# A graph layer on one core: row sums per relation in three groups of relations instead of two

## The chip, the core and the metric

One core of a Trainium2 chip runs the whole layer in one launch. The metric is the device time of one execution in microseconds (us); lower is better. Engines are named as in the profile: PE (TensorE, matrix products), DVE (VectorE), ACT (ScalarE), POOL (GpSimd) and SP (SyncE), each with its own instruction stream in program order. Engines wait for one another on semaphores.

## The reference, cut to what matters

```python
N, D, R, E = 1250, 1024, 8, 20000
xn = layernorm(x)
# graph part: one mean over incoming edges for each of 8 relations
out = xn @ root + bias
for r in range(8):
    mask = (edge_type == r)
    sums = segment_sum(xn[src] * mask, dst, num_segments=N)
    cnt = segment_sum(mask, dst, num_segments=N)
    out = out + (sums / max(cnt, 1)) @ weight[r]
u = out
z = concat([u, xn]) @ w_gate + b_gate
h = tanh(u) * z + xn * (1 - z)
x = x + h + linear_attention(xn)
x = x + fp4_ffn(layernorm(x))       # weights and activations quantized in blocks of 16
```

Edges come sorted by destination. On average a node has 16 incoming edges, 2 per relation.

## The kernel before, in words

The product is turned round: for each relation r the kernel first computes y_r = xn @ weight[r] for all nodes and stores it to memory (`relation_rows`), and the row of node n in `out` is then the sum over its edges of the row `src` of y_r, times 1/cnt. So the sums over edges need rows of products that are already stored.

**Steps.** PE runs 210 column steps (`NSTEP`). Step n is one tile of 128 nodes (n mod 10) times one block of weight columns (h = n // 10): h = 0 is q, k, v; h = 1 to 16 are the 8 relations, two halves of 512 columns each; 17 and 18 are root; 19 and 20 are the x part of the gate. A step is 24 matmuls of 128x512 (L1791: three products of high and low parts, eight k). ACT copies each step's result to EV and issues its store (L2166, L2168); from step 190 on DVE does the copy, with a bias (L1590). SP loads the weight rows (RAW, a ring of 4), ACT makes their high part (L2144), POOL their low part (L843 in `low_rows`), at t = n mod 10 = 1 to 8 for the block after. The engines' other work is hung on these steps: each engine's stream is written out step by step, so step numbers set the order within each engine.

**Edges.** From steps 10 to 19 DVE computes for each edge its place in a table of columns (`edge_words`, `edge_places`, `run_counts`): its running number among the edges of the same node in the same group of relations, and for the ones that do not fit a place among the columns left over. PE helps with small transposes at fixed places (`RUNS_AT`). Then `bucket_totals` on DVE counts edges by group and tile, one one-hot comparison and one sum per group. After that DVE makes the features for the attention keys, which PE takes from step 20 on (L1874). POOL scatters the edges' words to a table in memory (L922), and loads it back at step 75 (`LISTS_AT`). From step 79 (`COUNT_FROM`) PE counts left-over edges, one small matmul per left-over column after each k (`count_left`, L1838). At step `COUNTED_AT` (88 before) POOL stores the counts (L948), waits for them, and fetches the weights 1/cnt of the left-over columns with one indirect DMA per column (L894, `fetch_weights`), two columns per step.

**Groups, planes and left-over columns.** The relations are cut in groups. In each group and tile of 128 nodes there are `PLANES` columns of own rows (column c holds the node's c-th edge of the group, so partition p is node p) and `OVER` columns left over (any 128 edges of that tile and group). A column is an *item*. Each item is one indirect gather of up to 128 rows of 4 KB by POOL (L901) into one of 4 slots of `source_rows` (`RING`). A missing edge has an index out of bounds and moves no row.

- A plane takes one DVE instruction (L1548): u_sum = row * weight + u_sum.
- A left-over column takes a one-hot on DVE (L1528), a high part on ACT (L2226, `left_over_hi`), a low part on DVE (L1532), and four matmuls of 128x512 on PE (L1918, `aggregate`), hung at the last k of the step after the item's own. That is where PE waits for the item. Its slot is free when PE is done.
- When a tile's items are done, DVE adds the PSUM sums (L1558, `finish`), SP stores u_sum at place 2 of the next tile (L693). In all groups but the first, SP loads the sum so far of a tile at place 5 of the tile ahead (L689). In the last group root rows are added too (L1563).

Item m of a group has the step `AGG_FROM[g] + index * steps // items`; its gather stands in POOL's stream at the step of item m-4, behind that step's `low_rows`, and waits until item m-4 has let go of the slot. The groups' starts are `AGG_FROM`; a group's first gathers stand two steps ahead and need the group's last relation stored.

Other work on DVE: from step 118 (`QUANT_FROM`) the feed-forward weights are quantized, 24 pieces, at steps 2, 3 and 5 of each 7, up to step 173.

After step 209: PE multiplies u by its gate weights (L2034), and then the quantized feed-forward follows.

Of the kernel before, what the change touches and what calls it, by code (L numbers as in the profile page):

```python
# [25 lines left out]
R = 8  # L26
# [6 lines left out]

GROUPS = ((0, 5), (5, R))
NG = len(GROUPS)
PLANES = (8, 5)
OVER = (3, 2)
NBK = NG * NT  # L40
NPL = sum(PLANES) * NT
NOV = sum(OVER) * NT
NCOL = NPL + NOV
PLANE0 = [sum(PLANES[:g]) * NT for g in range(NG)]
OVER0 = [NPL + sum(OVER[:g]) * NT for g in range(NG)]
GCB = (11, 7)
NCH = sum(GCB) * NT
CHUNK0 = [sum(GCB[:g]) * NT for g in range(NG)]
ROUNDS_MAX = -(-E // (min(GCB) * P))
# [23 lines left out]
NSTEP = NT * NH  # L73
# [24 lines left out]
LISTS_AT = 75  # L98
COUNT_FROM = 79
COUNTED_AT = COUNT_FROM - (-NOV // KT) + 2  # L100
AGG_FROM = (117, 178, NSTEP)
QUANT_FROM, QUANT_STEPS = 118, 7


# [57 lines left out]
def gps_layer(nc, x, src, dst, edge_type_8, weight, root, bias, w_gate, b_gate, gamma, w_q, w_kv,  # L162
              w_out, ff_gate, ff_up, ff_down, out):
    with ExitStack() as ctx:
# [10 lines left out]

        y_d = [nc.dram_tensor(f"relation_rows{a}", [(b - a) * NP, D], F32).ap() for a, b in GROUPS]
        u_d = nc.dram_tensor("u_rows", [NP, D], F32).ap()
# [24 lines left out]
        zeros16 = keep("zeros16", [P, P], F16)  # L202
        bucket_ids = keep("bucket_ids", [P, len(GROUPS), NT], F32)
        round_edges = keep("round_edges", [P, len(GROUPS), ROUNDS_MAX], F32)
        norms = keep("norms", [P, NT], F32)
# [28 lines left out]
        e_tot = keep("edge_totals", [P, NBK], F32)  # L234
        e_end = keep("edge_ends", [P, len(GROUPS), NT + 1], F32)
        e_off = keep("edge_offsets", [P, NBK], F32)
# [113 lines left out]
        rc_out = sem("rc_out")  # L350
        weights_in = [sem(f"weights_in{j}") for j in range(len(GROUPS))]

# [460 lines left out]
        def _(pool):  # L813
# [114 lines left out]
            w_next = 0  # L928
            c_next = 0
            for n in range(NSTEP + 1):  # L930
                h, t = n // NT, n % NT
                if 1 <= t <= KT and n < NSTEP:
                    low_rows(KT * (h + 1) + t - 1)
                if n == SCATTER_FROM:
                    pool.wait_ge(words_ready, 1)
                if n >= SCATTER_FROM:
                    for c in range(c_next, min(c_next + SCATTER_EACH, EC)):
                        scatter(c)
                    c_next = min(c_next + SCATTER_EACH, EC)
                if n == LISTS_AT:  # L940
                    pool.wait_ge(mix_ps, NT)
                    for k in range(NLIST):
                        pool.wait_ge(listed[k], 16 * (EC // NLIST + 1))
                        g.dma_start(LISTS[:, k, :], list_d[k].rearrange(
                            "(p c) a -> p (c a)", p=P)).then_inc(lists_in, 16)
                if n == COUNTED_AT:
                    pool.wait_ge(lists_done, 1)
                    g.dma_start(rc_d.rearrange("(p c) a -> p (c a)", p=P), rcnt[:]).then_inc(rc_out, 16)  # L948
                    pool.wait_ge(rc_out, 16)
                if n >= COUNTED_AT:  # L950
                    for q in range(w_next, min(w_next + 2, NOV)):
                        fetch_weights(NPL + q, weight_at, q).then_inc(
                            weights_in[max(k for k in range(NG) if NPL + q >= OVER0[k])], 16)
                    w_next = min(w_next + 2, NOV)
                if n == AGG_FROM[0] - 2:
                    pool.wait_ge(mix_ps, NT)
                    g.memset(XG[:].rearrange("p s d -> p (s d)").bitcast(F32), 0.0).then_inc(xg_zero, 1)
                    pool.wait_ge(xg_zero, 1)
                for m in GATHERS_AT[n]:
                    gather(m)  # L960
# [1450 lines left out]
```

## Time and profile before

| | |
|---|---|
| runs | 1684.55, 1687.99, 1688.33 us; median 1687.99 |
| the profiled execution | 1685.22 us, of which its span is 1683.5 us |
| busy in the span | PE 1564.9 us (93%), DVE 902.8 (54%), POOL 784.0 (47%), ACT 403.2 (24%) |
| waits of PE, largest | 29.0 us for the low part of left-over columns (L1918, 18 times), 15.3 for hidden_t_lo, 12.3 and 12.1 for x at the start |
| DMA | 262.48 MB, mean 156 GB/s |

The profile counts an engine busy while an instruction of it is in work; matmuls overlap, so a busy PE hides gaps below about 0.2 us. PEclk is the granted clock of PE in tenths of full speed. Waits tell for whom an engine stood idle. Where the kernel is bound by PE, only time in which PE waits, runs at the lower clock, or has more matmuls counts.

### The profile page before, as it was taken

What the parts mean: (1) busy time and instruction counts of PE and PEld (TensorE: products, weight loads), DVE (VectorE), ACT (ScalarE), POOL (GpSimd) and SP (SyncE); (2) the same over time, 40 slices, a digit from 0 to 9 for tenths busy, and PEclk for the clock granted to TensorE, in tenths of its full rate; (3) what the DMA queues carried; (4) which work ended last, traced back from release to release, by engine and by line L of the source; (5) the groups of instructions that cost most, each with busy time, mean ns of one, the idle gap of its engine ahead of it and who ended that gap; (6) DMA issues with size and microseconds to landing.
All of it is one profiled execution on the core that took longest, in us unless ns stands there. A gap on an engine that the chain in (4) does not pass through costs nothing.

```text
span 1683.5 us, 19033 instructions
## 1 busy us (share of the span) xinstructions
PE 1564.9 (93%) x7138; PEld 1266.8 (75%) x7138; DVE 902.8 (54%) x1344; ACT 403.2 (24%) x595; POOL 784.0 (47%) x672
## 2 busy tenths in 40 slices
PE   4999999999999999999999999999899969977988
PEld 4987777777777688888778787777677758866887
DVE  6534223444432400006887788875677727777785
ACT  3321112222222121122222232232211122232220
POOL 4426766666662145644454464564555531211010
PEclk9999999999999999999999999999999979988999
DMA  4423333333323222237777777877887845440001
GB/s 156 141 93 83 84 91 85 110 99 98 104 89 101 76 85 82 94 116 236 256 256 246 245 254 260 264 244 254 319 272 270 296 179 189 151 136 7 31 38 47
DMA packets 120459, 262.48 MB, mean 156 GB/s; under 512 B 23451, under 2 KB 37010, under 8 KB 120360
## 3 DMA queue, kind: packets, MB, share of 16 engines
q1 hardware_dynamic: 48568, 109.34, 19.6%
q0 software_dynamic: 33056, 83.02, 16.5%
q10 hardware_dynamic: 38736, 68.83, 11.0%
q8 instruction: 58, 0.95, 0.2%
q14 instruction: 41, 0.34, 0.1%
HBM read 193.33 MB, written 80.06 MB: 162 GB/s over the span
## 4 chain that ended last, share of the span: by engine, by line
PE 62%; DVE 18%; DMA 9%; issue 5%; ACT 3%; POOL 2%; ACTq 0%; SPq 0%; POOLq 0%; DVEq 0%
PE ps L1791 46%; DMA source_rows<-relation_rows,row_list 6%; PE ps L2034 5%; DVE u_sum L1548 3%; PE ps L2066 2%; PE ps L1918 2%; PE ps L2084 2%; DVE source_rows L1532 1%; PE ps L1874 1%; PE ps L1898 1%; DMA u_sum<-u_rows 1%; PE ps L1910 1%; ACT source_rows_hi L2226 1%; DVE wq_rows L575 1%; DVE u_sum L1558 1%
## 5 line engine op out<-in xcount | busy, mean ns | idle before, releaser
L1791 PE MATMUL ps<-WH,XTH 128*128 128x512 f32 (+1 forms) x1680 | 667.0, 397 | 0.0
L1791 PE MATMUL ps<-WH,XTL 128*128 128x512 f32 (+1 forms) x1680 | 653.0, 389 | 0.0
L1791 PE MATMUL ps<-WL,XTH 128*128 128x512 f32 (+1 forms) x1680 | 652.7, 388 | 0.0
L1791 PEld LDWEIGHTS ps<-WH,XTH 128*128 128x128 f32 x1680 | 318.8, 190 | 65.1 <-issue 7.1
L843 POOL TENSOR_TENSOR WL<-RAW,WH 128x512 fp32r<-128x512 f32 (+1 forms) x184 | 239.1, 1303 | 275.8 <-ACT WH L2144 273.5
L1791 PEld LDWEIGHTS ps<-WH,XTL 128*128 128x128 f32 x1680 | 316.9, 189 | 64.5
L1791 PEld LDWEIGHTS ps<-WL,XTH 128*128 128x128 f32 x1680 | 317.7, 189 | 60.5 <-issue 2.4
L901 POOL DMA_INDIRECT source_rows<-relation_rows,row_list x180 | 223.3, 1241 | 265.7 <-PE ps L1918 119.4
L2166 ACT ACTIVATE EV<-ps 128x512 f32<-128x512 f32 x180 | 107.2, 595 | 582.7 <-PE ps L1791 511.1
L922 POOL DMA_INDIRECT edge_lists<-edge_words x160 | 196.9, 1231 | 46.3 <-issue 44.6
L1548 DVE SCALAR_TENSOR_TENSOR u_sum<-source_rows,weight_list,u_sum 128x1024 f32<-128x1024 f32 x120 | 169.8, 1415 | 77.4 <-DMA source_rows<-relation_rows,row_list 70.2
L1532 DVE SCALAR_TENSOR_TENSOR source_rows<-source_rows,weight_list,source_rows_hi 128x1024 fp32r<-128x1024 f32 x50 | 77.5, 1550 | 218.6 <-ACT source_rows_hi L2226 218.5
L2144 ACT ACTIVATE WH<-RAW 128x512 fp32r<-128x512 f32 (+1 forms) x184 | 115.1, 627 | 159.1 <-DVE EV L1590 74.7
L2226 ACT ACTIVATE source_rows_hi<-source_rows,weight_list 128x1024 fp32r<-128x1024 f32 x50 | 57.4, 1149 | 168.3 <-DMA source_rows<-relation_rows,row_list 138.2
L1493 DVE TENSOR_TENSOR prefix<-ps,qkv_tile 128x544 f32<-128x544 f32 x40 | 29.0, 724 | 110.5 <-PE ps L1898 110.5
L1009 POOL TENSOR_TENSOR xf<-xf,edge_words 128x1024 f32<-128x1024 f32 x10 | 19.4, 1940 | 138.2 <-DVE xf L1699 138.2
L2034 PE MATMUL ps<-WH,TH 128*128 128x512 f32 x160 | 65.6, 410 | 10.2 <-DVE TL L1649 10.2
L2034 PE MATMUL ps<-WL,TH 128*128 128x512 f32 x160 | 64.4, 402 | 0.0
L2034 PE MATMUL ps<-WH,TL 128*128 128x512 f32 x160 | 64.3, 402 | 0.0
L1918 PE MATMUL ps<-source_rows_hi,edge_one_hots 128*128 128x512 f32 x100 | 33.8, 420 | 29.1 <-DVE source_rows L1532 29.0
L894 POOL DMA_INDIRECT weight_list<-edge_weights,weight_at x50 | 50.2, 1005 | 15.4 <-issue 9.4
L1452 DVE COPY values<-qkv_tile 128x128 f32<-128x128 f32 x10 | 2.3, 227 | 93.2 <-PE ps L1878 93.1
(312 smaller groups left out, 1550.2 us busy)
## 6 DMA issues: line engine op xcount, KB each, us to landing
relation_rows<-EV ACTq DMA_DIRECT2D x160, 256.0 KB, 2.2
RAW<-in_L_gnn_weight SPq DMA_DIRECT2D x128, 256.0 KB, 2.9
u_rows<-u_sum SPq DMA_DIRECT2D x20, 512.0 KB, 5.4
RAW<-in_L_gnn_w_gate SPq DMA_DIRECT2D x32, 256.0 KB, 4.6
mix_rows<-mix_rows_out ACTq DMA_DIRECT2D x10, 512.0 KB, 2.6
root_rows<-EV ACTq DMA_DIRECT2D x20, 256.0 KB, 4.6
u_sum<-u_rows SPq DMA_DIRECT2D x10, 512.0 KB, 6.9
bias_rows<-root_rows SPq DMA_DIRECT2D x10, 512.0 KB, 7.0
```

What stands on the lines that cost most here:

```text
L843: g.tensor_tensor(WL[:, h % 2, k, 0:w], RAW[:, q % 4, 0:w], WH[:, h % 2, k, 0:w].bitcast(F32), ALU.subtract).then_inc(w_lo, 1)
L894: return g.indirect_dma_start(out=weight_list[:, to:to + 1], out_offset=None, in_=rc_d, in_offset=bass.IndirectOffsetOnAxis(ap=places[:, a ...
L901: return g.indirect_dma_start(out=XG[:, slot, :].bitcast(F32), out_offset=None, in_=y_d[group], in_offset=bass.IndirectOffsetOnAxis(ap=row ...
L922: g.indirect_dma_start(out=list_d[k], out_offset=bass.IndirectOffsetOnAxis(ap=ew[0:EP, SLOT, c:c + 1].bitcast(U32), axis=0), in_=ew[0:EP, ...
L1532: v.scalar_tensor_tensor(rows_, rows_.bitcast(F32), weight_list[:, m.column:m.column + 1], OHI[:].bitcast(F32), ALU.mult, ALU.subtract).th ...
L1548: v.scalar_tensor_tensor(acc[:], XG[:, m.index % RING, :].bitcast(F32), weight_list[:, m.column:m.column + 1], base[:], ALU.mult, ALU.add) ...
L1791: mm = t_.matmul(ps[:, bank, 0:w], a[:, t, k, :], b[:, s, k, 0:w], start=(k == 0 and j == 0), stop=(k == KT - 1 and j == 2))
L1918: mm = t_.matmul(ps[:, bank + b, :], S1H[:, one_hot, :], part[:, 512 * b:512 * b + 512], start=(first and j == 0), stop=(last and j == 1))
L2034: mm = t_.matmul(ps[:, 4 + 2 * s + b, :], a[:, s, k, :], w[:, h % 2, k, :], start=(k == 0 and j == 0), stop=(k == KT - 1 and j == 2))
L2144: a.activation(WH[:, h % 2, k, 0:w], raw, ACT.Copy).then_inc(w_hi, 1)
L2166: a.activation(ev_slot(s), ps[:, prod_bank(n), :], ACT.Copy).then_inc(ev, 1)
L2226: a.activation(OHI[:], XG[:, slot, :].bitcast(F32), ACT.Copy, scale=weight_list[:, m.column:m.column + 1]).then_inc(oh_hi, 1)
```

## The change

There are three groups of relations, 0 to 3, 4 to 5 and 6 to 7, with 8, 5 and 5 planes and 2, 1 and 1 left-over columns for each tile. Before there were two, 0 to 4 and 5 to 7, with 8 and 5 planes and 3 and 2 left over. So there are 180 planes and 40 left-over columns, 220 items, where there were 130, 50 and 180. The first group starts at step 93 instead of 117, the middle one at 147, the last one at 178 as before. Left-over weights are fetched four columns per step. `COUNTED_AT` follows from the number of left-over columns and becomes 86. `GCB` is a size of a general path that runs only when the edges do not fit the columns; the edges of the inputs fit in both versions (most left over in one tile and group: 177 of 256, 69 of 128 and 65 of 128; before 347 of 384 and 229 of 256).

```diff
--- before.py
+++ after.py
@@ -33,17 +33,17 @@
 
 
 
-GROUPS = ((0, 5), (5, R))
+GROUPS = ((0, 4), (4, 6), (6, R))
 NG = len(GROUPS)
-PLANES = (8, 5)
-OVER = (3, 2)
+PLANES = (8, 5, 5)
+OVER = (2, 1, 1)
 NBK = NG * NT
 NPL = sum(PLANES) * NT
 NOV = sum(OVER) * NT
 NCOL = NPL + NOV
 PLANE0 = [sum(PLANES[:g]) * NT for g in range(NG)]
 OVER0 = [NPL + sum(OVER[:g]) * NT for g in range(NG)]
-GCB = (11, 7)
+GCB = (9, 5, 6)
 NCH = sum(GCB) * NT
 CHUNK0 = [sum(GCB[:g]) * NT for g in range(NG)]
 ROUNDS_MAX = -(-E // (min(GCB) * P))
@@ -98,7 +98,7 @@
 LISTS_AT = 75
 COUNT_FROM = 79
 COUNTED_AT = COUNT_FROM - (-NOV // KT) + 2
-AGG_FROM = (117, 178, NSTEP)
+AGG_FROM = (93, 147, 178, NSTEP)
 QUANT_FROM, QUANT_STEPS = 118, 7
 
 
@@ -948,10 +948,10 @@
                     g.dma_start(rc_d.rearrange("(p c) a -> p (c a)", p=P), rcnt[:]).then_inc(rc_out, 16)
                     pool.wait_ge(rc_out, 16)
                 if n >= COUNTED_AT:
-                    for q in range(w_next, min(w_next + 2, NOV)):
+                    for q in range(w_next, min(w_next + 4, NOV)):
                         fetch_weights(NPL + q, weight_at, q).then_inc(
                             weights_in[max(k for k in range(NG) if NPL + q >= OVER0[k])], 16)
-                    w_next = min(w_next + 2, NOV)
+                    w_next = min(w_next + 4, NOV)
                 if n == AGG_FROM[0] - 2:
                     pool.wait_ge(mix_ps, NT)
                     g.memset(XG[:].rearrange("p s d -> p (s d)").bitcast(F32), 0.0).then_inc(xg_zero, 1)
```

**POOL, from the store of the counts to the first gathers.** Weight fetches are `weight_list<-edge_weights`, row gathers `source_rows<-relation_rows`, `WL<-RAW,WH` the low parts of weight rows. Before, at step 88 and at the end of the fetches, and then the first gathers of step 115:

```order
 L948 DMA edge_weights<-rcnt 128x80
 L894 DMA weight_list<-edge_weights,weight_at 128x1 x6
 L843 TENSOR_TENSOR WL<-RAW,WH 128x512
 L894 DMA weight_list<-edge_weights,weight_at 128x1 x2
 L843 TENSOR_TENSOR WL<-RAW,WH 128x512
 L894 DMA weight_list<-edge_weights,weight_at 128x1 x2
```

Now, from step 86 to step 96:

```order
 L948 DMA edge_weights<-rcnt 128x80
 L894 DMA weight_list<-edge_weights,weight_at 128x1 x4
 L843 TENSOR_TENSOR WL<-RAW,WH 128x512
 L894 DMA weight_list<-edge_weights,weight_at 128x1 x4
 L843 TENSOR_TENSOR WL<-RAW,WH 128x512
 L894 DMA weight_list<-edge_weights,weight_at 128x1 x12
 L843 TENSOR_TENSOR WL<-RAW,WH 128x512
 L894 DMA weight_list<-edge_weights,weight_at 128x1 x4
 L957 MEMSET source_rows 128x4096
 L901 DMA source_rows<-relation_rows,row_list 128x1024 x4
 L843 TENSOR_TENSOR WL<-RAW,WH 128x512
 L894 DMA weight_list<-edge_weights,weight_at 128x1 x4
```

Before, the 50 fetches were done long ahead of the first gather; now 24 of the 40 stand right ahead of it and 16 in between the first ones.

**DVE, in the placement of the edges (steps 16 to 19).** Names: `prefix`, `onehot` and `edge_words` are tables of 125 x 160 edges; L1083 is the third group's term in a table by group, L1317 and L1328 the one-hot and the sum of one group. One piece of the difference:

```order
 L1194 SCALAR_TENSOR_TENSOR edge_words<-prefix,unsorted 125x160
 L1080 TENSOR_SCALAR edge_words<-edge_words 125x160
+L1083 SCALAR_TENSOR_TENSOR edge_words<-edge_words 125x160
 L1325 TENSOR_TENSOR edge_words<-edge_words 125x160
+L1317 TENSOR_TENSOR onehot<-edge_words,bucket_ids 125x1600
+L1328 TENSOR_REDUCE edge_totals<-onehot 125x10
 L1317 TENSOR_TENSOR onehot<-edge_words,bucket_ids 125x1600
```

Three instructions are added here, two of them over 1600 elements; earlier in the same part each loop over groups has one more pass.

## Rows read from the trace of the kernel before

**Rows 1.** The page's chain of work that ended last, shares by engine.
```profile
PE 62%; DVE 18%; DMA 9%; issue 5%; ACT 3%; POOL 2%; ACTq 0%; SPq 0%; POOLq 0%; DVEq 0%
```

**Rows 2.** Waits of PE: us in total, times, longest; whole span, then 1148 to 1350.
```profile
PE ps L1918 <- DVE source_rows L1532: 29.0, 18, 3.3
PE ps L1918 <- DVE source_rows L1532: 16.6, 11, 3.3
```

**Rows 3.** Timeline of ACT: start us, us; evacuations after steps 79, 83, 90, 117, 178.
```profile
545.24 0.60 ACT L2166 ACTIVATE EV<-ps 128x512 f32<-128x512 f32 x1 [6.01 <-PE ps L1791]
571.69 0.60 ACT L2166 ACTIVATE EV<-ps 128x512 f32<-128x512 f32 x1 [4.93 <-PE ps L1791]
612.04 0.60 ACT L2166 ACTIVATE EV<-ps 128x512 f32<-128x512 f32 x1 [4.84 <-PE ps L1791]
758.92 0.60 ACT L2166 ACTIVATE EV<-ps 128x512 f32<-128x512 f32 x1 [2.57 <-PE ps L1791]
1137.56 0.60 ACT L2166 ACTIVATE EV<-ps 128x512 f32<-128x512 f32 x1 [2.71 <-PE ps L1791]
```

**Rows 4.** Timeline of DVE and PE, end of the edge placement.
```profile
116.45 0.55 DVE L1140 TENSOR_TENSOR_SCAN prefix<-prefix,run_carry 125x160 f32<-125x160 f32 x1
117.48 0.49 DVE L1143 TENSOR_TENSOR prefix<-prefix 125x320 f32<-125x320 f32 x1
126.37 0.32 DVE L1187 SCALAR_TENSOR_TENSOR prefix<-edge_words 125x160 f32<-125x160 f32 x1
130.33 1.83 DVE L1317 TENSOR_TENSOR onehot<-edge_words,bucket_ids 125x1600 f32<-125x1600 f32 x1
132.20 1.82 DVE L1328 TENSOR_REDUCE edge_totals<-onehot 125x10 f32<-125x1600 f32 x1
139.93 0.44 PE L1874 MATMUL ps<-onehot,qkv_tile 128*32 128x289 f32 x2 [0.59 <-DVE onehot L456]
```

**Rows 5.** Timeline of POOL: counts stored, weights fetched, first row gathers.
```profile
598.22 0.56 POOL L948 DMA_DIRECT2D edge_weights<-rcnt  x1
602.14 1.06 POOL L894 DMA_INDIRECT weight_list<-edge_weights,weight_at  x1 [3.37 <-DMA edge_weights<-rcnt]
603.51 1.02 POOL L894 DMA_INDIRECT weight_list<-edge_weights,weight_at  x1 [0.30 <-issue]
613.82 1.29 POOL L843 TENSOR_TENSOR WL<-RAW,WH 128x512 fp32r<-128x512 f32 x1 [4.07 <-ACT WH L2144]
745.59 3.53 POOL L957 MEMSET source_rows<- 128x4096 f32 x1
749.89 1.01 POOL L901 DMA_INDIRECT source_rows<-relation_rows,row_list  x1 [0.77 <-POOL source_rows L957]
```

**Rows 6.** Timeline of DVE and PE, first left-over column.
```profile
756.38 2.07 DVE L1532 SCALAR_TENSOR_TENSOR source_rows<-source_rows,weight_list,source_rows_hi 128x1024 fp32r<-128x1024 f32 x1 [153.15 <-ACT source_rows_hi L2226]
764.16 0.39 PE L1918 MATMUL ps<-source_rows_hi,edge_one_hots 128*128 128x512 f32 x1
```

**Rows 7.** Instructions of source_rows: ns min/median/max; waiters; landing times.
```profile
L901 POOL DMA_INDIRECT source_rows<-relation_rows,row_list x180: 986/1008/2056, 749.9 to 1340.3; - x180
L1548 DVE SCALAR_TENSOR_TENSOR u_sum<-source_rows,weight_list,u_sum x120: 1267/1285/3044, 763.9 to 1348.8; 128x1024 f32<-128x1024 f32 x120
...
  POOL source_rows L901: 239.8, 77
...
DMA to landing us min/median/max: 3.2/5.9/10.7
```

**Rows 8.** Windows of 10 us: busy (x) by engine, PEclk, DMA share, GB/s.
```profile
805.00:815.00 10.00, 7.62 (x27) 5.79 (x26) 6.25 (x7) 1.85 (x4) 5.88 (x6) 0.83 0.93 307
```

**Rows 9.** Window of DVE: length, busy (x), PEclk, DMA share, GB/s.
```profile
765.00:970.00 205.00, 160.64 (x217) 0.98 0.76 246
```

**Rows 10.** Timeline of PE and DVE, end of the last step.
```profile
1344.41 0.39 PE L1791 MATMUL ps<-WH,XTL 128*128 128x512 f32 x1
1350.01 0.68 DVE L1590 TENSOR_TENSOR EV<-ps,z_bias 128x512 f32<-128x512 f32 x1
```

## The prediction

> **What bounds the kernel now.** I read the chain of work that ended last first. PE carries 62% of it and nothing else more than 18% [rows 1], so a change counts by what PE does, waits for, or runs slower at. The waits of PE come next: the largest are 29.0 us, 18 times, up to 3.3 us, for the low part of a left-over column [rows 2]. That is the one place at which the sums over edges hold PE. Then the marks of the steps in ACT's timeline. From step 90 to 117 PE needs (758.92 - 612.04)/27 = 5.44 us a step [rows 3], with nothing to wait for: the plain price of a step, 24 matmuls of 0.227 us. From 117 to 178 it takes 378.64 us for 61 steps. The plain price is 331.8, and the 30 left-over columns have four matmuls each, 0.91 us, 27.3 in all, so 19.5 us are lost. From 178 to the last product at 1344.6 [rows 10] there are 31 steps, 168.6 us, and 20 columns, 18.1, of 207.1 us: 20.4 lost. So 39.9 us are lost while items run. 29.0 are the waits, and the rest is mostly the clock: in the 10 us from 805 PE waited 2.4 us and the granted clock was 0.83 [rows 8], a level of 1.2 GHz for part of that window, which is 1.7 us more; I count four windows like it, some 7 us.
>
> Why the waits: a left-over column keeps its slot until the end of the step after its own. POOL stands at the gather of item m+4 until then (in all it was held 239.8 us in 77 places by source_rows [rows 7]), and that gather lands 5.9 us (median) later. When item m+4 is itself left over, it reaches PE just in time or late. Before, two of three left-over columns in the first group and half in the second follow at distance 4 (places 0, 3, 7 of 11; 0, 3 of 7).
>
> **The change part by part**, against the profiled execution's 1685.2 us (span 1683.5).
>
> *Placement of the edges, DVE.* What comes before DVE's last wait for PE in this part is hidden: DVE stood idle there. After it, at 116.3, all is in one line, and PE takes the first key features at 139.93 after 0.59 us of waiting [rows 4]: the line has no slack. The third group adds one scan pass (a scan is 0.55, some 0.5 in line), four instructions over all groups' elements that grow by half (0.49 for 320 elements, so about 0.17 each), one more multiply-compare (0.3), five L1083 (each 0.32 and a semaphore, 0.36, by L1187), and one pair L1317 and L1328 (1.83 + 1.82, 3.7 with gaps). Sum 0.5 + 0.7 + 0.3 + 1.8 + 3.7 = 7.0, with loose ends 7.1 us. All of it becomes a wait of PE at step 20. Next late: nothing, since in the key steps DVE idles until PE is done with each tile. **+7.1.**
>
> *Counting left-over edges.* Steps with these matmuls take (571.69 - 545.24)/4 = 6.61 us [rows 3], 1.17 over the plain price for eight: 0.146 each. Ten fewer: **-1.5.** The longer tables (220 columns for 180) add a microsecond to DVE before PE's first count, and PE did not wait there.
>
> *Matmuls of left-over columns.* Ten fewer at 0.91 us (PE's four from 764.16 [rows 6]): **-9.1.** Fifty more planes are DVE's, 40 more gathers POOL's. The rows moved stay one per edge, 20000 of 4 KB; only ten more loads and stores each of u_sum are added, over 117 steps instead of 93. So transfers per step fall, and I take landing times as before.
>
> *The start of the first group.* This is the queue of POOL. Let T be the start of step 86. POOL reaches the store of the counts at T + 3.0, and the first weight fetch comes 3.9 us later [rows 5], at T + 6.9. A fetch takes 1.31 us in line (1.02 and a gap of 0.30), a low part 1.29 and 1.43 with the gap behind it. Four fetches end at T + 12.2; steps 87 and 88 with a low part and four fetches add 6.65 each, to 25.5; steps 89 and 90 add 5.2 each, to 35.9; step 91 to 42.6. The memset and its wait are 4.3 (745.59 to 749.89), so the first gather is issued at T + 46.9. Before, from that issue to the end of the low part took 8.6 us (749.89 to 756.38 + 2.07 [rows 5, 6]), which gives T + 55.5. PE is at that column's place nine steps after T, at 49.0: it waits 6.5. Before, the same column was ready at 758.45 and PE came at 764.16. Behind the four gathers (52.1) stand steps 92 and 93 with eight more fetches (65.4) and then gathers 4 and 5. Item 5 is left over: issued 66.7, ready 75.3, PE there at 59.8 + 0.9 + 6.5 = 67.2, so it waits 8.1. Steps 94 and 95 bring POOL to 86.4, gather 10 goes out at 87.8, ready 96.4, PE there at 76.2 + 1.8 + 14.6 = 92.6: 3.8. After that POOL has 1.4 + 2 x 1.3 = 4.0 us of work in a step of 5.44 and catches up; item 15 is in time. Sum **+18.4.** With the shortest landing (3.2 against the 5.3 assumed) it is 16.3, with the longest (10.7) 23.8 [rows 7].
>
> POOL's gather instruction has a median of 1.008 us and a maximum of 2.056 [rows 7]; at the start DVE has little to do, and I priced it at the quiet pitch. The Trainium skill, "GPSIMD Engine Reference", section Specifications, says that GpSimd shares its SBUF interface with VectorE and contends with DVE instructions that read two SBUF inputs. The plane's multiply-add is one, and the change adds fifty. By the quiet row the start costs 18.4; by the rule, with each of the ten gathers concerned half way to the maximum of its row, it would be 5 more.
>
> *Waits while items run.* After the start 37 left-over columns remain. In the second and third group they are 6 items apart, 3.1 steps: the late item m+4 lands about 3.3 steps after m, and item m+6 is due at PE 5 steps after, nearly a step of slack. In the first group they are 5 apart; where that falls on two steps (about six times) the slack is about 1.5 us, otherwise a step more. The nearest rows are 16.6 us in 20 columns, 0.83 each, for the last group before, and with the other 12.4 in 30, 0.41 each, for the first [rows 2]. The bounds are 0 and 0.83 each: 0 to 31 us. I take 0.25, 9 us: six tight columns at the old rate or a little more, and some for the middle stretch, where DVE is fullest. 9 for 29: **-20.**
>
> *Clock.* Four waits of over 3 us (step 20 and the start) and one later at 1.7 us, against four before: **+1.7.**
>
> *The last step.* PE's last product ended at 1344.6, but DVE put its copy behind the last planes, which waited for their gathers, until 1350.01 [rows 10]; the rest hangs on that copy's store. With 1.9 items a step for 2.2 these gathers come in time: at most 5.1 us gained, I take **-4.**
>
> Sum: 1685.2 + 7.1 - 1.5 - 9.1 + 18.4 - 20 + 1.7 - 4 = 1677.8. The profiled execution lies 2.8 us below the median of the runs, and 1.3 below the mean of all four. I forecast 1679 us.
>
> **The rivals.**
> *DVE becomes the bound in the middle stretch (slower).* Between 765 and 970 DVE was busy 160.64 of 205 us [rows 9], 4.9 us in a step of 6.2. From step 147 to 173 a step has 0.14 more items (0.2 us) and 0.16 more tile ends (0.2): 5.25 us for a step that should take 5.73. It decides from the point where quantization, which comes in bursts, holds DVE for more than the one step of slack. Then the old rate of 0.83 us per column goes on: 31 us instead of 9, 1700 us. For it: 92% load. Against it: a step more of slack than before at a similar load.
> *Half of the waits stay (no change).* 19 us instead of 9, by late loads of u_sum, which now have two items of time (5.9 us) between issue and use, where three were: 1688.
> *The start costs nothing (much faster).* If POOL gets to the first gathers in time, 18.4 and the three clock windows (5.1) fall away: 1654. Against it stand 24 fetches at a measured pitch in front of them.
>
> **How the numbers follow.** A measurement of this kernel tells about 0.3%, 5 us, from no change. My forecast has 0.49, DVE as the bound 0.25, half of the waits 0.18, the free start 0.08. The forecast's own range is 1665 to 1683: waits of 0 and 15, a start of 16.3 and 23.8. For 8 in 10 I take 1662 to 1700: it leaves out most of the free start and the part of the slow case above 1700. Faster by over 0.3%: 0.57; within: 0.18; slower: 0.25.
>
> **What would show it.** The first wait of PE at L1874 is 7 to 8 us. Three waits at L1918 of about 6.5, 8 and 4 us lie at steps 95 to 100, with POOL never idle between the first weight fetch and gather 10. Later waits at L1918 sum to about 9. The last copy by DVE starts within 2 us of PE's last product. I am wrong if the waits between steps 147 and 178 exceed 8 us, if ACT or the weight rows (w_lo) hold PE after the start, or if the first gather goes out before step 94.

## The result, and the profile after

| | before | after |
|---|---|---|
| median of five runs | 1687.99 us (1678.0 to 1690.69) | 1701.53 us (1698.17 to 1704.51) |
| ratio to before | | 1.0086, 95% interval 1.0066 to 1.0105 |
| profiled execution, and its span | 1685.22, 1683.5 us | 1704.51, 1702.6 us |

The changed kernel is 0.9% slower. The forecast was 1679 us in a range of 1662 to 1700, so it had the wrong sign, and the time lies above the range. The profiled executions are 19.3 us apart, the medians 13.5, since the one of before was a little fast and the one of after a little slow; the working below is in profiled executions.

I read the new profile in the order of the old one. First the page's chain of work that ended last, by engine:

```profile
PE 49%; DVE 21%; DMA 10%; issue 10%; POOL 7%; ACT 3%; ACTq 0%; SPq 0%; POOLq 0%; DVEq 0%
```

PE had 62% of it [rows 1]. It now has 49%, and what took its place is POOL, DVE, transfers, and "issue", time in which an engine waited for nothing that the profile shows. The clearest place is the start: from 550 to 700 the chain was PE alone before, and now has 21% in POOL's weight fetches and 22% in "issue".

Then the waits of PE (total, times, longest), in the whole span, then the stretches 643 to 700, 795 to 976, 976 to 1175 and 1175 to 1369, that is the start of the first group, its rest in steps 118 to 146, and the second and third group:

```profile
PE ps L1918 <- DVE source_rows L1532: 47.7, 20, 6.0
PE ps L1874 <- DVE onehot L456: 6.7, 1, 6.7
...
PE ps L1918 <- DVE source_rows L1532: 15.5, 3, 6.0
...
PE ps L1918 <- DVE source_rows L1532: 7.8, 5, 3.8
...
PE ps L1918 <- DVE source_rows L1532: 18.1, 6, 6.0
...
PE ps L1918 <- DVE source_rows L1532: 6.3, 6, 2.1
```

There are 40 left-over columns for 50, but 47.7 us of waiting for them instead of 29.0 [rows 2].

Then the marks of the steps: ACT's evacuations after steps 79, 117 and 178, and DVE's last copy.

```profile
552.41 0.60 ACT L2166 ACTIVATE EV<-ps 128x512 f32<-128x512 f32 x1 [6.01 <-PE ps L1791]
794.66 0.60 ACT L2166 ACTIVATE EV<-ps 128x512 f32<-128x512 f32 x1 [0.82 <-PE ps L1791]
1180.59 0.60 ACT L2166 ACTIVATE EV<-ps 128x512 f32<-128x512 f32 x1 [1.76 <-PE ps L1791]
...
1368.87 0.68 DVE L1590 TENSOR_TENSOR EV<-ps,z_bias 128x512 f32<-128x512 f32 x1
```

Set beside the same marks of before [rows 3, 10], they say where the 19.1 us of span went:

| stretch | before | after | difference |
|---|---|---|---|
| start to step 79 | 545.2 | 552.4 | +7.2 |
| 79 to 117 | 213.7 | 242.3 | +28.6 |
| 117 to 178 | 378.6 | 385.9 | +7.3 |
| 178 to the last copy | 212.5 | 188.3 | -24.2 |
| behind it | 333.5 | 333.7 | +0.2 |

The last stretch gained 24 us, as was hoped: 9 of them are the matmuls of ten left-over columns, 10 are waits. The edge placement and the start of the first group took 36, and the middle, which should have given back, took 7 more. The second and third rows hide a shift: nine left-over columns, 8 us of matmuls, now stand before the mark of step 117. Without it the start lost some 22 us and the stretch from 117 to 178 some 15.

### The profile page after: what moved, and what is told of

Same layout as the page of the kernel before. It is cut to its first block, busy times and chain, and to the rows that moved or that the text cites. A ratio compares the mean times of both kernels' runs of the same rounds, so it can differ in the third digit from the quotient of the medians.

```text
span 1702.6 us, 19114 instructions
## 1 busy us (share of the span) xinstructions
PE 1560.4 (92%) x7088; PEld 1262.4 (74%) x7088; DVE 984.5 (58%) x1392; ACT 392.8 (23%) x585; POOL 827.9 (49%) x703
## 4 chain that ended last, share of the span: by engine, by line
PE 49%; DVE 21%; DMA 10%; issue 10%; POOL 7%; ACT 3%; ACTq 0%; SPq 0%; POOLq 0%; DVEq 0%
PE ps L1791 35%; PE ps L2034 5%; DMA source_rows<-relation_rows,row_list 4%; DVE u_sum L1548 3%; DMA u_sum<-u_rows 3%; POOL WL L843 2%; POOL source_rows L901 2%; PE ps L2066 2%; POOL weight_list L894 2%; PE ps L1874 1%; PE ps L1918 1%; PE ps L2084 1%; PE ps L1898 1%; DVE wq_tmp L565 1%; PE ps L1910 1%
## 5 line engine op out<-in xcount | busy, mean ns | idle before, releaser
L901 POOL DMA_INDIRECT source_rows<-relation_rows,row_list x220 | 269.0, 1223 | 302.2 <-DVE u_sum L1548 138.4
L1548 DVE SCALAR_TENSOR_TENSOR u_sum<-source_rows,weight_list,u_sum 128x1024 f32<-128x1024 f32 x170 | 242.1, 1424 | 136.1 <-DMA source_rows<-relation_rows,row_list 97.0
L1532 DVE SCALAR_TENSOR_TENSOR source_rows<-source_rows,weight_list,source_rows_hi 128x1024 fp32r<-128x1024 f32 x40 | 69.0, 1726 | 102.1 <-ACT source_rows_hi L2226 102.1
L2226 ACT ACTIVATE source_rows_hi<-source_rows,weight_list 128x1024 fp32r<-128x1024 f32 x40 | 46.0, 1150 | 156.0 <-DMA source_rows<-relation_rows,row_list 156.0
L1918 PE MATMUL ps<-source_rows_hi,edge_one_hots 128*128 128x512 f32 x80 | 28.5, 439 | 47.7 <-DVE source_rows L1532 47.7
L1918 PEld LDWEIGHTS ps<-source_rows_hi,edge_one_hots 128*128 128x128 f32 x80 | 14.1, 198 | 57.3 <-issue 41.6
```

The costliest lines, as they stand in the source:

```text
L901: return g.indirect_dma_start(out=XG[:, slot, :].bitcast(F32), out_offset=None, in_=y_d[group], in_offset=bass.IndirectOffsetOnAxis(ap=row ...
L1532: v.scalar_tensor_tensor(rows_, rows_.bitcast(F32), weight_list[:, m.column:m.column + 1], OHI[:].bitcast(F32), ALU.mult, ALU.subtract).th ...
L1548: v.scalar_tensor_tensor(acc[:], XG[:, m.index % RING, :].bitcast(F32), weight_list[:, m.column:m.column + 1], base[:], ALU.mult, ALU.add) ...
L1918: mm = t_.matmul(ps[:, bank + b, :], S1H[:, one_hot, :], part[:, 512 * b:512 * b + 512], start=(first and j == 0), stop=(last and j == 1))
L2226: a.activation(OHI[:], XG[:, slot, :].bitcast(F32), ACT.Copy, scale=weight_list[:, m.column:m.column + 1]).then_inc(oh_hi, 1)
```

## The experiments

Each is an edit of the changed kernel (e) or of the kernel before (b). Each batch was timed beside the kernel before on its chip, and comparisons go by the ratio to it: 0.001 is 1.7 us, and the changed kernel stands at 1.0086. A difference from the changed kernel joins two such ratios, each good to about 0.002, so it is uncertain by some 4 us. Waits are those of the one profiled execution of each kernel. An added line moves lines below it by one, so L1919 and L1533 in some profiles are L1918 and L1532 here.

**e1: fewer weight fetches ahead of the first gathers.** Once the weights of the first group's 20 left-over columns are in, one fetch per step.

```diff
-                    for q in range(w_next, min(w_next + 4, NOV)):
+                    some = 4 if w_next < NT * OVER[0] else 1
+                    for q in range(w_next, min(w_next + some, NOV)):
...
-                    w_next = min(w_next + 4, NOV)
+                    w_next = min(w_next + some, NOV)
```

> The changed kernel, with one edit: the 20 weights of the first group are fetched four per step as before, the 20 of the other two groups one per step after that. Theory POOL's queue: the first row gather is issued 5.2 - 1.3 = 3.9 us earlier, steps 92 to 95 of POOL are 3.9 us shorter each, so the first wait of PE at L1918 is about 0 (3.9 before), the next two (5.6 and 6.0) are gone, with the clock windows some 17 us of the 22.3 us lost in steps 86 to 102: 1685 us. Rival, that latency of the gathers themselves makes these waits: under 5 us gained.

Measured: 1683.74 us, ratio 0.9989 (0.9974 to 1.0004), so 16 us less than the changed kernel. POOL's first gather of the changed kernel and of this one:

```profile
636.03 1.00 POOL L901 DMA_INDIRECT source_rows<-relation_rows,row_list  x1 [0.77 <-POOL source_rows L957]
```

```profile
633.32 1.01 POOL L901 DMA_INDIRECT source_rows<-relation_rows,row_list  x1 [0.77 <-POOL source_rows L958]
```

It goes out 2.7 us sooner, and 4.2 counted from the start of step 86 (3.9 was expected), which takes away the first wait. The rest of the 16 us comes behind it, where single fetches stand between the gathers instead of groups of eight. PE waited 1.5 us where it had waited 15.5, and steps 86 to 102 took 97.6 us for 117.6. The middle and the end stayed much as they were (17.4 and 5.7 us of waits). The start is a loss of its own, of the size and from the queue that the prediction named.

**e2: quantization earlier,** in steps 91 to 146 instead of 118 to 173, so that it is over before the second group.

```diff
-QUANT_FROM, QUANT_STEPS = 118, 7
+QUANT_FROM, QUANT_STEPS = 91, 7
```

> The changed kernel, with one edit: quantization of the feed-forward weights runs from step 91 to 146 instead of 118 to 173, so the middle stretch (147 to 177) has none of it. Theory DVE's load: the 18.1 us of waits at L1918 in the middle stretch fall below 4, those in the first group after step 118 (7.8) stay or grow by some us, and the kernel is 8 to 14 us faster than the changed one: 1690 us. Rival, the loads of u_sum that stand behind weight rows on SP: the middle stretch keeps most of its 18.1 us, within 5 us of 1701.

Measured: 1686.57 us, ratio 1.0006 (0.9990 to 1.0022), 13.5 us less. Waits of PE in its steps 147 to 177 (978 to 1154):

```profile
PE ps L1918 <- DVE source_rows L1532: 1.3, 1, 1.3
```

and these steps took 175.9 us where they took 199.6. With DVE free the middle stretch is not late, though DVE waited longer there for loads of u_sum than in the changed kernel (15.1 us):

```profile
DVE u_sum L1548 <- DMA u_sum<-u_rows: 27.8, 9, 5.4
```

So late loads alone hardly reached PE in this run; in e6 below they cost more.

**e3: u_sum stored and loaded one place earlier by SP.** In the last group the load of the root rows stands with the store and moves too.

```diff
-                    if m.place == 2 and m.sum > 0:
+                    if m.place == 1 and m.sum > 0:
...
-                    if m.place == 5 and NT <= m.sum + 1 < NBK:
+                    if m.place == 4 and NT <= m.sum + 1 < NBK:
```

> The changed kernel, with one edit on SP: u_sum is stored at place 1 of the next tile and loaded at place 4 (2 and 5 before), one item earlier each. Theory late loads of u_sum: DVE's waits for them (11.1 us in the middle stretch, 18.9 in the last one) fall by half or more, the waits of PE in the middle stretch from 18.1 to under 10, 8 to 12 us faster than the changed one: 1691 us. Rival DVE's load by quantization: PE's waits stay within 3 us, 1700 us.

Measured: 1689.25 us, ratio 1.0022 (1.0007 to 1.0038), 10.8 us less. PE's waits in the middle fell from 18.1 to 11.1 us (under 10 was expected), those of the last group from 6.3 to none, and DVE's for u_sum from 15 to 3 and from 15 to 0.4. So the late loads do cost, in part of the middle and, with the root rows, in the last group.

**e4: only two groups' edge totals.** The third group's totals are set to zero instead of counted (its part of the table by tile is left out; the edges of these inputs fit and do not need it).

```diff
-                for j in range(NG):
+                v.memset(e_tot[0:EP, 2 * NT:3 * NT], 0.0)
+                for j in range(2):
...
-                    if j < NG - 1:
+                    if j < 1:
```

> The changed kernel without the count of edges of the third group (its totals are set to zero; they only decide whether the general path runs, so no output changes). One one-hot comparison and one sum less on DVE: the wait of PE at L1874 falls from 6.7 us by 3.7 to 3.0 if this line of DVE is all that PE waits for; if something else released it, it stays.

Measured: PE's wait for the first key features, of the changed kernel and of this one:

```profile
PE ps L1874 <- DVE onehot L456: 6.7, 1, 6.7
```

```profile
PE ps L1875 <- DVE onehot L456: 3.0, 1, 3.0
```

3.7 us, the price set for the pair L1317 and L1328 from [rows 4], to a tenth. Its one run took 1697.91 us, which alone is too near to the others' spread to show it.

**e5: the three edits together.**

> The changed kernel with all three edits together: one weight fetch per step once the first group's are in, quantization from step 91, and SP's store and load of u_sum one place earlier. Theory (three separate losses, each freed by its own edit): the start's loss falls from 22 to about 5 us (quantization now shares these steps, so not to 2), the waits of PE at left-over columns in steps 146 to 177 from 18 to about 1, and those of the last stretch from 6 to about 0; of the 48 us of waits less than 10 stay, and the time is 1660 us, 1655 to 1668. Rival (the losses are one slack passed on: what one edit frees, the next stage takes): at best the single edits' 1684 us, 1680 to 1687, with 25 us of waits or more left.

Measured: 1669.78 us, ratio 0.9900 (0.9873 to 0.9927). Faster than before, but 10 us short of the theory. The middle and the last group behaved (0 and 2.1 us of waits); the start did not. Its wait of PE, and DVE's rows ahead of it:

```profile
PE ps L1919 <- DVE source_rows L1533: 13.0, 1, 13.0
```

```profile
648.04 1.28 DVE L1549 SCALAR_TENSOR_TENSOR u_sum<-source_rows,weight_list,bias_rows 128x1024 f32<-128x1024 f32 x1 [6.78 <-DMA bias_rows<-in_L_gnn_bias]
649.24 0.51 DVE L555 TENSOR_REDUCE wq_scale<-wq_rows 128x22 f32<-128x352 f32 x1
...
655.27 2.67 DVE L1549 SCALAR_TENSOR_TENSOR u_sum<-source_rows,weight_list,u_sum 128x1024 f32<-128x1024 f32 x2
657.86 0.51 DVE L555 TENSOR_REDUCE wq_scale<-wq_rows 128x22 f32<-128x352 f32 x1
...
665.11 1.28 DVE L1533 SCALAR_TENSOR_TENSOR source_rows<-source_rows,weight_list,source_rows_hi 128x1024 fp32r<-128x1024 f32 x1
```

DVE's first plane waited until 648.04 for the bias rows, which SP loads at the step before the group's start, behind weight rows that wait for POOL. Two pieces of quantization of 6.0 and 5.8 us, with two planes between them, stand in the program between that plane and the second left-over column, and delayed it to 665. An idle engine would have done them for nothing; behind a late plane they were the path.

**b1, b2: the same edits without the change,** on the kernel before with its two groups.

> The kernel before, two groups, with quantization from step 91, so that most of it runs in steps in which DVE has no items. Theory (a DVE full of quantization makes left-over columns late): the 12.4 us of waits in the first group fall below 5 and the 16.6 us of the last group stay; time 1677 us, 1672 to 1682. Rival (before, the waits come from the distance of four items between left-over columns alone, DVE has room): waits 12 and 17 as before, time unchanged, 1684 to 1689.

> The kernel before, two groups, with quantization from step 91 and SP's store and load of u_sum one place earlier. Theory (late loads of u_sum are a part of what holds DVE in the last group): 5 us less than the same without the earlier loads, about 1672 us, waits in the last group 16.6 to about 11. Rival (the last group's waits come from the distance between left-over columns): they stay at 15 us or more and the time is that of quantization early alone, about 1677. Either way it is the two-group kernel to set beside the three-group one with the same edits: three groups are worth their 7 us of edge placement only if that one is faster by more than 5 us.

Measured: b1 1677.87 us, ratio 0.9953 (0.9937 to 0.9969); b2 1672.92 us, ratio 0.9919 (0.9892 to 0.9945). In b1 the waits of the first group fell from 12.3 to 6.3 us (under 5 was expected) and those of the last stayed at 16.4. Only 11 of the 24 pieces ran ahead of the first group, not most of them as the expectation has it, and the 6.3 us all lie beside the other 13; steps 147 to 177, with no piece left, had none. So at least half of the first group's waits before were quantization's, and the last group's were not. In b2 the last group's fell to 11.4, where 11 was expected. But DVE had waited only 0.5 us there for u_sum in b1, and 1.0 in b2, so it is not the shorter wait for the load that gained them; the earlier store and the shifted root loads move too, and which of these did it stays open.

**e6: quantization without its work.** Each piece is replaced by one copy onto itself; transfers and waits stay. (The expectation says 16 us of DVE for a piece. That is the price of the three pieces of a round of seven steps; the 24 pieces together took 132 us, 5.5 each.)

```diff
-                    ch = Chain(dve, dve_q, (3 * r + m) * QSTEPS)
-                    quantize(v, ch, WQI[:, m, :], WQT[:], WQS).then_inc(wq_done, 1)
+                    v.tensor_copy(WQI[:, m, :], WQI[:, m, :]).then_inc(wq_done, 1)
```

> The changed kernel with each quantization of a piece of the feed-forward weights, some 16 us of DVE's work, replaced by one copy of the piece onto itself; its transfers and waits stay where they were, and the feed-forward uses unquantized weights. Theory (it is DVE's load that makes the middle stretch late): waits of PE at left-over columns in steps 146 to 177 fall from 18.1 to under 3 us, the start's 15.5 stay, time 1681 us, 1677 to 1686. Rival (the transfers and the waits of ACT around a piece, or SP's late loads of u_sum, make it late, not the load of DVE): over 10 us of waits stay there, and the time is 1690 us or more.

Measured: 1677.10 us, ratio 0.9942 (0.9920 to 0.9964), 24 us less. Steps 118 to 146 came down to the plain price, 168.1 us without a wait, where they had 180.9. The middle stretch kept 6.4 us of its 18.1, more than the theory's 3. Waits there of PE, and of DVE for u_sum (the edit takes a line away, so that L1917 is L1918 here):

```profile
PE ps L1917 <- DVE source_rows L1532: 6.4, 4, 2.8
...
DVE u_sum L1548 <- DMA u_sum<-u_rows: 36.7, 9, 6.4
```

**e8: the same, and u_sum one place earlier,** to tell whether what stayed were the loads of u_sum or quantization's transfers.

> The changed kernel with each quantization of a piece replaced by one copy onto itself (the feed-forward uses unquantized weights), and SP's store and load of u_sum one place earlier. Without the second edit 6.4 us of PE's waits stayed in steps 146 to 177, beside 36.7 us in which DVE waited for loads of u_sum. Theory (DVE's load and the late loads together make the middle stretch late): waits of PE there 0 to 1 us, DVE's for u_sum under 5, time 1671 us, 1665 to 1678. Rival (what stays is the transfers and ACT's waits around each piece): 4 us or more stay there.

Measured: 1661.71 us, ratio 0.9849 (0.9829 to 0.9868), 16 us below e6 and at the lower end of what was expected. PE waits at no left-over column after the start; DVE's waits for u_sum in the middle are 9.7 us (under 5 was expected), and harmless. The window of the middle stretch, 964 to 1142 (length, then busy PE, PEld, DVE, ACT, POOL with counts, PEclk, DMA share, GB/s), against 976 to 1160 of the changed kernel, shown first:

```profile
976.00:1160.00 184.00, 165.91 (x707) 135.03 (x706) 153.80 (x193) 41.80 (x62) 96.23 (x78) 0.97 0.75 249
```

```profile
964.00:1142.00 178.00, 178.00 (x787) 147.23 (x786) 113.27 (x94) 45.15 (x67) 109.97 (x86) 1.00 0.82 277
```

PE busy for all of 178 us at the full clock, with quantization's transfers still there and more bytes per second than before: neither the transfers nor the DMA load make this stretch late by themselves.

**e7: all three edits, clear of the start.** Quantization from step 98, and the bias rows loaded five steps earlier.

```diff
-QUANT_FROM, QUANT_STEPS = 91, 7
+QUANT_FROM, QUANT_STEPS = 98, 7
...
-                if n == AGG_FROM[0] - 1:
+                if n == AGG_FROM[0] - 6:
```

> The changed kernel with all three edits, but quantization from step 98, so that it keeps clear of the first group's first items, and SP's load of the bias rows, which DVE waited 6.8 us for in the same kernel with quantization from step 91, five steps earlier. Theory (the 13.0 us wait of PE at the first items came from quantization pieces that stood in DVE's queue between planes that the bias had made late): that wait falls below 2 us, the other waits at left-over columns stay at 10 us or less, and the time is 1660 us, 1655 to 1665. Rival (three edits together leave no slack, and the loss comes up elsewhere, now in steps 147 to 154, where the last pieces meet the second group): 1667 us or more, with the new waits there.

Measured: 1658.82 us (1656.82 to 1664.18), ratio 0.9834 (0.9820 to 0.9849). Its page's chain, and PE's waits at left-over columns in the whole span:

```profile
PE 61%; DVE 20%; DMA 7%; issue 5%; POOL 4%; ACT 2%; ACTq 0%; SPq 0%; POOLq 0%; DVEq 0%
```

```profile
PE ps L1919 <- DVE source_rows L1533: 16.0, 12, 2.1
```

The profiled execution is the slowest of the five, 1664.18 us. The 13.0 us wait is gone: 0.7 us of waits stay up to step 102. In all 16.0 us stay, more than the 12 or less expected, most of them (11.6) in steps 103 to 146, where quantization runs beside the eight planes of the first group, and none is over 2.1 us. The time is what the theory gave.

**e9: the same with quantization from step 91 again,** so that only the earlier bias rows set it apart from e5.

> The changed kernel with fetches late, quantization from step 91, u_sum earlier, and the bias rows five steps earlier, to tell which of the last two edits took away the 13.0 us wait at the start. Theory (the late bias made the first plane late, and only behind it did two pieces of quantization stand in the way of the second left-over column): without the late bias DVE does its first plane 6.8 us sooner, the wait falls to 13.0 - 6.8 = about 6 us or less, and the time is 1663 us, 1659 to 1667. Rival (it is quantization in these steps, whatever the bias): the wait stays at 10 us or more and the time at 1668 to 1671. Second rival (the bias alone): under 1 us of waits, and 1659 us as with quantization from step 98.

Measured: 1663.78 us (1659.99 to 1667.66), ratio 0.9879 (0.9851 to 0.9907). The wait of 13.0 us at the start is now

```profile
658.18 1.22 PE L1919 MATMUL ps<-source_rows_hi,edge_one_hots 128*128 128x512 f32 x2 [6.33 <-DVE source_rows L1533]
```

as the theory had it: the bias's 6.8 us passed to PE in full, since quantization stood behind it, and the other half is quantization by itself.

**b3: the two-group kernel with three of the four edits:** quantization from step 91 (11 of its 24 pieces are ahead of its first group), u_sum and the bias rows earlier.

> The kernel before, two groups, with quantization from step 91, u_sum's store and load one place earlier, and the bias rows loaded five steps earlier. Its first group waits for the bias only where PE does not wait for DVE, so both theories expect the 1673 us that it had without the last edit, 1669 to 1676. It is the best two-group kernel of this study: by the theory of separate losses the three-group one beats it by 10 us or more, by the rival by 5 us or less.

Measured: 1668.73 us (1667.23 to 1671.71), ratio 0.9901 (0.9885 to 0.9917), just below what was expected. 9.5 us of its waits are in the last group and 5.9 in the first, most of them beside the 13 later pieces. The three-group kernel of e7, timed beside it, is 0.0067, 11 us, faster. That is between these two kernels: neither is known to be the best of its kind, and a two-group kernel with all of quantization ahead of its first group was not run.

## Why the prediction was wrong, point by point

**Right: the edge placement.** +7.1 was forecast. The first key features waited 6.7 us for 0.6, 6.1 more, and step 79 came 7.2 us later; the rest is PE's matmuls behind the wait, which ran at the lower clock for a while and which the prediction has in its clock term. e4 confirms the largest part, 3.7 us.

**Right: the count and the matmuls.** -1.5 and -9.1. Steps with counting took the same 6.61 us, and PE's other products did not change.

**Right, by its own sum: the start.** Waits of 6.5, 8.1 and 3.8 us were forecast, 18.4 in all, and 3.9, 5.6 and 6.0 measured, 15.5 in all; the first gather stood 46.0 us behind the start of step 86 where 46.9 was worked out. The single waits were each off by 2 to 3 us, two down and one up, so that their sum fits is in part luck. With the lower clock that followed the waits (0.89 from 617 to 695), steps 86 to 102 lost 22.4 us over their plain price of 92.5 and three columns. The prediction has 18.4 and three windows of 1.7, 23.5. e1 gave 16 us back.

The queue was priced at the quiet pitch. It held for the 24 fetches ahead of the first gather (1.30 to 1.37 us apart where no low part stood between) and for the first ten gathers (0.99 to 1.00 each). Of the 16 fetches among the gathers, with DVE at work, eight took 1.08 to 1.82 us for 1.00, 3.2 us more in all. The dearer estimate, 5 us by the Trainium skill, "GPSIMD Engine Reference", section Specifications (GpSimd and VectorE share an SBUF interface), is met in part by its size, on the fetches and not on the gathers. No run shows that it was this interface that stretched them, and the waits stayed below the quiet sum.

**Wrong: the waits while items run.** This is the step that failed: "I take 0.25, 9 us", one of two bounds, chosen by the distance between left-over columns. After the start 32.2 us of waits came, 0.87 for each of 37 columns, and with them 5 us more of lower clock and small gaps than the prediction allowed. That is 28 us, and the forecast missed the profiled execution by 1704.5 - 1677.8 = 26.7; the rest (the last copy, which gained 2.4 us instead of 4, and the start) nearly cancels. The prediction's own sign of being wrong, more than 8 us of waits between steps 147 and 178, came with 18.1. The upper bound, 0.83 from the last group of before [rows 2], fits the mean, but by chance: the waits were 7.8 us in 17 columns of the first group (0.46 each), 18.1 in ten of the second (1.81) and 6.3 in ten of the third (0.63). The middle stretch was under-priced most, some 4 us for 18.1. The narrower range, "1665 to 1683", does not follow from its own terms either: waits of 0 and 15 us and a start of 16.3 and 23.8 give 1668 to 1691.

Why the distance did not help is a circle of three queues. From 1095 on, in the changed kernel, POOL, SP, DVE, and PE at the end:

```profile
1099.85 1.29 POOL L843 TENSOR_TENSOR WL<-RAW,WH 128x512 fp32r<-128x512 f32 x1
1107.56 1.50 POOL L901 DMA_INDIRECT source_rows<-relation_rows,row_list  x1 [6.42 <-DVE u_sum L1548]
...
1110.46 1.65 POOL L843 TENSOR_TENSOR WL<-RAW,WH 128x512 fp32r<-128x512 f32 x1
```

```profile
1101.54 0.63 SPq L693 DMA_DIRECT2D u_rows<-u_sum  x1
1112.14 4.88 SPq L632 DMA_DIRECT2D RAW<-in_L_gnn_root  x2
1117.07 0.49 SPq L689 DMA_DIRECT2D u_sum<-u_rows  x1
```

```profile
1105.50 5.45 DVE L1548 SCALAR_TENSOR_TENSOR u_sum<-source_rows,weight_list,u_sum 128x1024 f32<-128x1024 f32 x4 [2.48 <-DMA u_sum<-u_rows]
...
1124.65 2.67 DVE L1548 SCALAR_TENSOR_TENSOR u_sum<-source_rows,weight_list,u_sum 128x1024 f32<-128x1024 f32 x2 [5.76 <-DMA u_sum<-u_rows]
1127.24 0.51 DVE L555 TENSOR_REDUCE wq_scale<-wq_rows 128x22 f32<-128x352 f32 x1
...
1131.72 2.67 DVE L1548 SCALAR_TENSOR_TENSOR u_sum<-source_rows,weight_list,u_sum 128x1024 f32<-128x1024 f32 x2
1134.31 0.51 DVE L555 TENSOR_REDUCE wq_scale<-wq_rows 128x22 f32<-128x352 f32 x1
...
1141.56 1.28 DVE L1532 SCALAR_TENSOR_TENSOR source_rows<-source_rows,weight_list,source_rows_hi 128x1024 fp32r<-128x1024 f32 x1
```

```profile
1142.98 1.19 PE L1918 MATMUL ps<-source_rows_hi,edge_one_hots 128*128 128x512 f32 x2 [5.97 <-DVE source_rows L1532]
```

A gather on POOL waits until DVE has done its plane; the low part of the weight rows stands behind that gather; SP's next weight rows wait for the low part, and the load of u_sum stands behind them; DVE's next plane waits for that load. Then quantization, two pieces of 4.4 and 5.8 us with two planes between, stands in front of the next left-over column, and PE waited 5.97 us for it at 1142.98. With room, DVE catches up: in e2 it waited 27.8 us for these loads in the middle and PE only 1.3. With quantization in steps 147 to 173 it has no such room.

**How the rivals fared.** "DVE becomes the bound in the middle stretch" had 0.25 and 1700 us. In the middle stretch it is what happened, and the deciding point was as stated: quantization in bursts holding DVE longer than the slack. That its total price came out too is luck: it spread 31 us evenly over all columns, as the upper bound did. "Half of the waits stay, by late loads of u_sum" is its second half: e2 and e6 show that late loads with a free DVE cost 1.3 and 6.4 us in the middle (quantization is elsewhere in e2; in e6 its transfers stay; what makes the 5 us between the two is not shown). e3 shows that a full DVE with loads in time costs 11.1, and e8 that with neither there is no wait. The whole is one loss with two handles: both edits reach the middle, and each of them gives its own part elsewhere. "The start costs nothing" was false for the kernel as changed.

**The weighing that went wrong.** The trace had the load: 4.9 of 6.2 us [rows 9] and 5.25 of 5.73 worked out, 92%; from 976 to 1060 it was 89%. Against it stood "a step more of slack", worked out for a gather that is issued when its slot is free. That slack assumes that DVE reaches each item at once. With pieces of 5.5 us in its queue, up to two within one step and a half, the step of slack, 5.44 us, is spent by one piece. That number could be had from the trace of before, where the 24 pieces are 128.9 us, 5.4 each, but the prediction does not have it.

**Open.** ACT too stands for quantization: it stood idle from 1093.07 to 1103.06, 10 us, until it could store a round's pieces, with high parts and evacuations behind it. e6 and e8 take this wait away together with the load of DVE, so its share of the middle stretch's 18 us is not told apart.

## What to carry to other kernels

Slack that is worked out from the distance between items says little when an instruction group in the queue of the engine that serves them is as long as that slack, as here: compare the slack with the longest burst, not with the mean load. Where in-order queues wait for one another in a circle (here POOL's gathers, SP's loads, DVE's sums), one late link is repeated at each turn, and a store and a load moved ahead in their queue by one place were worth 11 us (e3), 16 (e8 against e6) and 6 (b2 against b1). A change that shifts work into a stretch should be tried with the neighbours shifted as well: here the same regrouping was 0.9% slower alone and, with four small edits around it, 0.7% faster than two groups with three of these edits.

## What the runs showed of the hardware that was not expected

DVE's small instructions were stretched beside POOL's work. The 24 of each kind in quantization show it (ns min/median/max), in the changed kernel:

```profile
L573 DVE TENSOR_TENSOR wq_rows<-wq_rows,wq_scale x24: 524/526/2399, 814.1 to 1148.7; 128x352 f32<-128x352 f32 x24
L565 DVE TENSOR_SCALAR wq_tmp<-wq_rows x24: 343/345/1882, 814.7 to 1149.2; 128x352 int32<-128x352 int32 x24
L577 DVE TENSOR_TENSOR wq_rows<-wq_rows,wq_scale x24: 524/526/528, 816.6 to 1152.9; 128x352 f32<-128x352 f32 x24
```

The longest are 1.5 to 1.9 us over the median. In all, 20 of the 240 instructions took over 0.4 us more than their median. Each of the 20 has the same rows of POOL beside it: a gather in work when it starts, a low part right behind the gather, and its own end up to 0.4 us behind the end of that low part. Two examples of 0.34 us otherwise took 1.99 us from 1099.36 and 1.83 from 1136.23, and ended at 1101.35 and 1138.06, each 0.2 us behind the end of a low part of POOL (1099.85 + 1.29 and 1136.57 + 1.29): as if they had stood until it was done. L577 was spared in this kernel, but took up to 2.00 us in the kernel before. DVE's own low part of a left-over column (L1532) took 1726 ns in the mean where its quiet form takes 1.28 us.

That agrees in part with the Trainium skill, "SBUF — State Buffer", section Summary: rules for kernel authors, where of two such instructions of DVE and GpSimd the second to issue is blocked until the first is done. The Trainium skill asks there for a two-port mode, or for two SBUF inputs beside a GpSimd instruction that reads SBUF (the low part does). L573, L575 and L576 have two inputs; L557, L565 and L566 have one, and no run shows their mode. By the rows the DVE instruction starts 0.3 to 0.7 us ahead of the low part, during the gather, so they do not show which was the second to issue. It means that DVE pays too: a piece takes 5.5 us on average where the shortest of its ten instructions add up to 3.9. No run here separates this from other causes.

PE's clock did not follow the length of a wait alone. In the changed kernel, behind the wait of 3.16 us at 1096.35 the second pair of matmuls of L1918 took 0.62 us, as at the full clock, 2.4 GHz. Behind those of 4.05 us at 1117.91 and 6.00 at 688.62 it took 1.05, and the windows around them show a granted clock of 0.95 (1109 to 1142) and 0.89 (617 to 695), that is 1.2 GHz for a part of each. But in e3 the pair behind a wait of 3.58 us took 0.63, and in b1 those behind waits of 2.86 and 2.82 took 1.05. Nor do the totals show that long waits cost more for their length: the 47.7 us here came with 17.5 us of other losses, the 29.0 of before with 10.9, 0.37 and 0.38 for each us.
